# Additions of early expert rows in groups instead of one by one, with spare rows for each of a group

## What is computed

```python
xn = layernorm(x)
x  = x + gat(xn, edges, ...) + linear_attention(xn, ...)
xf = layernorm(x)
top_w, top_i = top_k(xf @ Wg + bg, 2)
w_dense = sum(one_hot(top_i, 8) * softmax(top_w)[..., None], axis=1)
for e in range(8):
    h = gelu(xf @ W1[e] + b1[e])
    out = out + w_dense[:, e:e+1] * (h @ W2[e] + b2[e])
return x + out
```

## Time and profile before

| | |
|---|---|
| median of 3 runs | 967.84 us (967.2 to 976.45) |
| profiled execution | 969.72 us |
| its span | 967.4 us |
| mean granted clock of PE | 0.924 |
| PE busy | 811.3 us (84%) |
| POOL busy | 563.4 us (58%) |
| DVE busy | 531.8 us (55%) |
| DMA into `out` in the chain that ended last (L1060's) | 20% of the span |

### The profile page before, as it was taken

The page is one execution under the profiler, slowest core; times in us unless marked ns, Lnnn a source line. Parts: engine busy times, 40 slices in busy tenths (PEclk is TensorE's granted clock), DMA queues, the critical chain, the costliest instruction groups (busy, mean ns, idle before and its releaser), DMA issues.

```text
span 967.4 us, 17943 instructions
## 1 busy us (share of the span) xinstructions
PE 811.3 (84%) x4901; PEld 703.3 (73%) x4902; DVE 531.8 (55%) x1485; ACT 424.8 (44%) x1126; POOL 563.4 (58%) x580
## 2 busy tenths in 40 slices
PE   8986676777677468878798897799999999999995
PEld 7884454555456347767687776699999999999994
DVE  6789787887776787668567767741111111111111
ACT  4656433443443247666655742533333333333330
POOL 2077777777777777777777777364333343343331
PEclk9998999798776779999889878999999999999998
DMA  8347544554456445756656575964556566556561
GB/s 239 111 133 238 142 136 137 144 153 135 129 161 192 129 130 157 240 174 191 207 168 171 152 226 121 317 207 84 173 167 203 172 168 202 172 172 200 171 167 18
DMA packets 80183, 162.18 MB, mean 168 GB/s; under 512 B 11569, under 2 KB 46278, under 8 KB 79989
## 3 DMA queue, kind: packets, MB, share of 16 engines
q1 hardware_dynamic: 49029, 91.06, 29.2%
q0 software_dynamic: 30528, 69.83, 28.6%
q10 hardware_dynamic: 560, 0.52, 0.2%
HBM read 144.12 MB, written 17.25 MB: 167 GB/s over the span
## 4 chain that ended last, share of the span: by engine, by line
DMA 28%; POOL 20%; issue 17%; DVE 17%; PE 14%; DVEq 3%; POOLq 1%; ACT 0%; ACTq 0%
DMA out<-one_hot 20%; POOL gathered L1000 17%; DVE gathered L2024 5%; DVE acc L1993 3%; PE bank L1569 3%; DMA out<-w_sb,add_l 3%; DMA gathered<-h_table,src_row 3%; PE bank L1385 2%; PE bank L1556 2%; PE bank L1742 1%; DVEq L1987 1%; DMA gathered<-xn_table,one_hot 1%; PE bank L1652 1%; DMA w_sb<-in_L_gnn_att_dst 1%; DVE z L2012 1%
## 5 line engine op out<-in xcount | busy, mean ns | idle before, releaser
L1000 POOL DMA_INDIRECT gathered<-h_table,src_row x416 | 400.6, 963 | 128.4 <-issue 125.1
L1569 PE MATMUL bank<-gathered,one_hot 128*128 128x260 f32 x832 | 249.0, 451 | 126.1 <-DVE acc L1993 123.7
L1569 PEld LDWEIGHTS bank<-gathered,one_hot 128*128 128x128 f32 x832 | 175.5, 222 | 174.0 <-DVE acc L1993 144.0
L1346 ACT ACTIVATE one_hot<-bank,one_hot 128x128 f32<-128x128 f32 x312 | 89.0, 368 | 183.7 <-PE bank L1722 183.7
L1060 POOL DMA_INDIRECT out<-one_hot x39 | 61.2, 1568 | 170.2 <-DMA out<-one_hot 111.7
L1722 PEld LDWEIGHTS bank<-one_hot,acc 128*128 128x128 f32 x1248 | 145.5, 192 | 2.7 <-ACT one_hot L1338 0.8
L1722 PE MATMUL bank<-one_hot,acc 128*128 128x128 f32 x1248 | 145.9, 275 | 0.5 <-ACT one_hot L1338 0.5
L1742 PE MATMUL bank<-w_sb,one_hot 128*128 x624 | 141.2, 380 | 0.0
L2024 DVE TENSOR_TENSOR gathered<-gathered,bank 128x1024 f32<-128x1024 f32 x104 | 127.0, 1221 | 3.2
L1742 PEld LDWEIGHTS bank<-w_sb,one_hot 128*128 128x128 f32 x624 | 115.8, 190 | 14.3 <-issue 0.2
L1993 DVE TENSOR_TENSOR acc<-acc,bank 64x260 f32 x208 | 87.9, 423 | 69.2 <-issue 55.6
(11 more groups left out here) (363 smaller groups left out, 1035.7 us busy)
## 6 DMA issues: line engine op xcount, KB each, us to landing
acc<-in_L_ffn_W SPq DMA_DIRECT2D x40, 1024.0 KB, 5.1
w_sb<-in_L_ffn_W SPq DMA_DIRECT2D x16, 1024.0 KB, 10.7
w_sb<-key_table SPq DMA_DIRECT2D x52, 256.0 KB, 3.6
gathered<-h_table,src_row POOLq DMA_INDIRECT x416, 3.1
h_table<-acc SPq DMA_DIRECT2D x25, 130.0 KB, 2.0
xs<-in_L_ffn_W SPq DMA_DIRECT2D x3, 1024.0 KB, 12.2
out<-xs SPq DMA_DIRECT2D x5, 512.0 KB
xn_table<-w_sb SPq DMA_DIRECT2D x5, 512.0 KB, 5.1
```

The costliest lines, as they stand in the source:

```text
L1000: pool.indirect_dma_start(gathered[:, r, j, :], None, h_table, bass.IndirectOffsetOnAxis(ap=src_row[:, t:t + 1], axis=0)).then_inc(gather_ ...
L1346: op = act.activation(hiddenT[:, k, g * P:(g + 1) * P], hidden_bank[2 * k + half][:, f * P:(f + 1) * P], ACT.Gelu, bias=b1_slot[:, k, g:g ...
L1569: mm = pe.matmul(sum_bank[r % SUMS][:, 0:ROW], one_hot[:, r, j, :], gathered[:, r, j, :], start=(j == 0), stop=(j == G - 1))
```

## The change

Additions of tiles of one expert no longer wait for each other. `add_rows(u)` waits only for the additions up to the last even u (so 1, 3, 5, 7 and 9 have no wait on `y_added`), `add_early(u)` only for those ahead of its expert's first tile (so 1 and 2, 4 and 5 have none beyond that). The steps of the tile loop wait as before. So that two additions in flight don't meet in a spare row, `out` gets 3 x 128 spare rows, the tiles of an expert use different blocks of them, SP clears three blocks, and the two DVE operations that build the spare row numbers take them from a table of three columns.

On all five engines the instructions stand in the same order as before. What differs is that POOL's additions with u of 1, 3 and so on lose their wait or wait for a smaller count, that two operations of DVE have another form, that an iota has three columns, and that SP issues three stores where it issued one.

```diff
-SPARE = P
+SPARES = 3
+SPARE = SPARES * P
...
+        spare_id = gat_bias_sb[:, P + NT + NX:P + NT + NX + SPARES]
...
-                sp.dma_start(out[N:N + SPARE, :], acc[:, NB, 0:D]).then_inc(zeros_in, 16)
+                for k in range(SPARES):
+                    sp.dma_start(out[N + k * P:N + (k + 1) * P, :], acc[:, NB, 0:D]).then_inc(zeros_in, 16)
...
-                pool.iota(row_id[:, :], [[0, 1]], base=N + 1, channel_multiplier=1,
+                pool.iota(spare_id[:, :], [[P, SPARES]], base=N + 1, channel_multiplier=1,
...
                 def add_rows(u):
-                    if u:
-                        pool.wait_ge(y_added, u * 16)
+                    if u >= LD:
+                        pool.wait_ge(y_added, u // LD * LD * 16)
...
                 def add_early(u):
-                    pool.wait_ge(y_added, (u + NL) * 16)
+                    pool.wait_ge(y_added, (u // DEPTH * DEPTH + NL) * 16)
...
-                        dve.tensor_scalar(none_l, token_l, 0.0, row_id[:, 0:1], ALU.is_equal, ALU.mult).then_inc(early_step, 1)
+                        dve.scalar_tensor_tensor(out=none_l.rearrange("p (e j) -> p e j", e=LX), in0=token_l.rearrange("p (e j) -> p e j", e=LX),
+                                                 scalar=0.0, in1=spare_id[:, 0:LD].unsqueeze(1).broadcast_to((P, LX, LD)),
+                                                 op0=ALU.is_equal, op1=ALU.mult).then_inc(early_step, 1)
...
-                        dve.tensor_scalar(none_there, token_a, 0.0, row_id[:, 0:1], ALU.is_equal, ALU.mult).then_inc(early_step, 1)
+                        dve.scalar_tensor_tensor(out=none_there.rearrange("p (e j) -> p e j", e=FIRST), in0=token_a.rearrange("p (e j) -> p e j", e=FIRST),
+                                                 scalar=0.0, in1=spare_id[:, 0:DEPTH].unsqueeze(1).broadcast_to((P, FIRST, DEPTH)),
+                                                 op0=ALU.is_equal, op1=ALU.mult).then_inc(early_step, 1)
```

More of the change, by code:

```diff
@@ L890, in _ @@
                     sp.dma_start(w1_slot[:, u, :, :], first_layer(sp, u)).then_inc(w1_in[u], 16)
-                sp.wait_ge(zeros_in, 16)
+                sp.wait_ge(zeros_in, SPARES * 16)
                 def step(u, k, ahead):
@@ L1012, in read_early @@
                                             bass.IndirectOffsetOnAxis(ap=read_a[:, u:u + 1], axis=0)).then_inc(xga_in[u // 4], 16)
-                pool.wait_ge(zeros_in, 16)
+                pool.wait_ge(zeros_in, SPARES * 16)
                 pool.wait_ge(scalar_l, passes * EVENTS)
@@ L2350, in _ @@
                 dve.wait_ge(kv_in, 64)
-                dve.wait_ge(zeros_in, 16)
+                dve.wait_ge(zeros_in, SPARES * 16)
                 with dve.Fori(0, passes) as c:
```

## The result

Over 20 runs of each, side by side, the changed kernel takes 967.80 us at the median and the kernel before 972.03. The ratio is 0.9963, with a 95% interval of 0.9948 to 0.9978, that is 3.6 us faster (2.1 to 5.1). (The ratio is not formed from the two medians, which differ by 4.2 us.) The forecast was 1.3 us, to 966.5. One of the changed kernel's 20 executions took 1085.09 us, with a mean granted clock of 0.723 instead of some 0.926; it is left out of the ratio. The profiled executions don't show the difference (970.23 us after, 969.72 before).

The account below looks back on a forecast made before the run. The prediction took PE, full from 700 to 940 us, to bound the last stretch, so only PE's idling before the tile loop counted. Terms of -1.07 and -0.26 with costs 0 gave -1.3 us, 967.84 to 966.5; range 964.2 to 969.4.

Parts of the forecast that it names:

- Term (a): Before the first placement: additions 4 and 5 overlap, 6 starts at 618.1 instead of 624.10, PE gains 1.07 us.
- The rival of additions in series: Before the first placement: additions in flight run in series, 6 starts at 623.6, gain 0.5 and 0.26 us, 967.1; chance 0.15.
- ScalarE is late next: At the first placement: with POOL early, ScalarE's share ends at 625.87 and PE starts at 625.96 instead of 627.03.
- PE's wait of 1.6 us: Sign of being right: PE's wait before the first placement is 1.6 us, ended by ScalarE.
- the 2.69 us of the old wait: Before the first placement: PE waits 2.69 us for POOL's first weave, which stands behind addition 6; read from one profile.
- Term (b): Tile loop's start: first addition starts at 683.5 instead of 685.68, and PE's 0.26 us wait for a late read goes.
- Terms (c): Costs of zero stores, iota, two DVE forms (each 0 to 0.25 us) and earlier SP loads, all taken as 0.
- The slower rival: Tile loop: reads behind additions late in every tile, 9.4 us less the 1.07, giving 976.2; chance 0.04.
- The rival of a tile loop paced by additions: Tile loop: the chain of additions sets its pace, not PE, so the end moves 2.2 us, to 965.6; chance 0.08.
- No effect: First placement: PE's wait was for ScalarE all along, so the time stays 967.8; chance 0.11.

Follow-up runs that it names:

- pairs only: The changed kernel with the six additions of experts 0 and 1 waiting one by one again; 0.9971 of the kernel before, 968.56 us against 971.45.
- threes only: The changed kernel with the ten additions of the loop's tiles waiting one by one again; 0.9999 of the kernel before.
- shares_first: The changed kernel with ScalarE's shares(0) moved ahead of early_rows(2); 0.9925 of the kernel before, 964.24 us against 971.37.
- shares_first_serial: The kernel before, all additions one by one, with ScalarE's shares(0) moved ahead of early_rows(2); 0.9992 of the kernel before.

## Why the prediction was right, and where its size was off

**Which stall, and what bounds behind it.** Right. Of the ways an addition could reach PE, the one before the first placement carries what is measurable: pairs only gives 0.9971, threes only 0.9999, and one more landing ahead of the weave costs 8.2 us. PE is full in the tile loop as the earlier trace rows had it, and POOL's 102.6 us of waits there still cost nothing.

**Term (a), the additions.** The working came out: 4 at 608.88 (608.2), 5 at 610.75 (610.1), 6 at 618.43 (618.1). The two transfers lie side by side. (The first weave started at 623.79 instead of 622, because DVE's table and PE's transposes came some 2 us later in this execution, 625.96 against 623.96 for the transposes.) The rival of additions in series has fallen: 618.43 - 610.75 = 7.7 us, as much as one alone took in the earlier trace rows. That 7.7 is the low end, though: in the other five profiles with pairs, from the start of 5 to that of 6 takes 8.1 to 9.0 us. From the start of addition 4 to that of 6 it is 9.6 to 10.9 us in the six profiles with pairs and 13.9 to 16.9 in the seven where 6 follows in series ahead of the first weave. The Trainium skill's rule that each DMA engine goes round its queues by packets (DMA: Bandwidth & Descriptors, "Queues, rings and completion order") leaned toward that rival. By the times just given it can have cost a pair's second addition about a microsecond. That ScalarE is late next is shown by shares_first, where its move takes the wait away, and PE's wait of 1.6 us was measured as 1.72 or 1.73 in all five profiles with pairs and ScalarE's old order.

**The step that was off: the 2.69 us of the old wait.** The prediction took it from one profile and let it stand for the kernel. In the four profiles with the old waits ahead of the placements and nothing moved, it is 2.69, 4.18, 2.94 and 2.41 us, 3.06 at the mean, since it hangs on landings in series in full DMA engines. Against 1.72 that makes 1.3 us instead of 1.07. And in two of the four the clock falls behind it, 1.63 us each, 0.8 at the mean, which the prediction had at nothing; with 1.72 us it fell in none of five. Together 2.1 us. This is rough. Three of the four profiles are of executions 4 to 5 us above their kernel's median (975.66, 975.61 and 974.7 us). And shares_first_serial, whose additions go in series too, waited only 1.49 us for DVE and would have waited 1.7 for ScalarE in its old order; with it as a fifth the two terms are 1.1 and 0.65 us, together 1.7, an estimate from these rows. The five measurements of kernels with pairs and ScalarE's old order gave 0.9963, 0.9971, 0.9962, 0.9983 and 0.9977 of before, 0.9971 at the mean or 2.8 us; two of the five intervals reach just above 1 (1.0008 and 1.0002). The forecast of 1.3 was too small by about half of those 2.8 us. The old wait and its clock account for 1.7 to 2.1 us of them, and the cause of the rest is open. A second error lay in the starting point: three runs gave 967.84 where 20 gave 972.03, 4.2 us too low. A gain too small puts the forecast too high and a start too low puts it too low, so 966.5 came near the measured 967.80 by luck, by two errors of opposite sign.

**Term (b), the tile loop's start.** The addition does start earlier, 0.82 us behind DVE as worked out. PE's late read at the third tile did go: it stands there, with 0.17 to 0.32 us, in five of the eight profiles whose early additions go one by one ahead of the tile loop, pairs only among them, and in none of the six with threes. But the changed kernel has one of 0.33 us at another tile instead (709.45 us), and the length of the tile loop does not show the difference (290.31 in pairs only, 290.49 and 290.25 in the changed kernel). The sum should have had 0.

**Terms (c).** The costs were 0 as far as can be measured: spare rows alone, with the output's size and the DVE forms, gave 1.000 (0.9981 to 1.002).

**The slower rival, late reads in the tile loop.** It did not come from the change, yet the thing exists: 3.1 and 3.8 us in two of the eight profiles with additions in series before the placements, in none of the six with pairs. One of the two had the early additions in threes and one did not, so these don't decide it. What decides it is open: fourteen profiles are too few to say that the pairs prevent it, and no run here changed the reads. If they do, it would be part of the gain: over the four profiles of the table above with additions in series the mean of the sums is 336.6 us against 332.5 in the five with pairs and ScalarE's old order, 4.1 us and more than the 2.8 that were measured. This rival to my account of the size is not excluded.

**The rival of a tile loop paced by additions** has fallen: apart from the two profiles with late reads, the loop's length is 289.8 to 290.6 us whether its first addition waits for DVE or for a landing. **No effect** has fallen with the interval of the main comparison (0.9948 to 0.9978).

## What to carry to other kernels

A wait of the bottleneck engine has to be read from several executions before it is priced: this one varied from 2.4 to 4.2 us between profiles of the same waits, and those of 2.94 us and more cost more than their length, as PE's clock fell too. Where a queue in program order holds both transfers and work that others wait for, let only the issue of a transfer stand ahead of that work, never its landing, and then look who is late next: here one line moved on ScalarE was worth about as much again, and nothing measurable without the first step. Moving one landing behind the first weave only brought its wait back at the second placement and the fifth.

## What the runs showed of the hardware that was not expected

TensorE idle for 2.94, 4.18 and 9.90 us was followed by sixteen products of 3.50, 2.95 and 2.72 us instead of 1.96 and a granted clock of 0.79, 0.79 and 0.76 in the next 8 us, at 1.6 to 1.8 us in all; idle for 2.69 us and less before the first placement it was not. In the two shorter of these the clock fell 1.3 and 0.5 us after TensorE had resumed. Two indirect additions into `out` in flight on one queue, beside loads that keep the DMA share near 1, took 9.6 to 10.9 us from the first's start until a third could start behind both, where two in series took 13.9 to 16.9. And the landing of such reads and additions differs between executions of one program: in one the medians in the tile loop were 6.3 us for additions and 4.7 for reads, in another 3.9 and 5.5.
